# The last tiles of a token pipeline: seven loop passes written out as one order per engine

## The reference, cut to what matters

```python
h = _layernorm(x) * (1 + ca) + sa
x = x + ga * attn(h)            # the token stage
h = _layernorm(x) * (1 + cb) + sb
x = x + gb * experts(h)         # the expert stage
# attn(x):
h = rms_norm(x, ln1_w); xx = shifted(h) - h
r, k, v, g, w = five mixtures of h and xx, each times a matrix
S = dt * S + k * v              # a scan over the tokens, 16 heads of 8 x 8
o = r * (S + u * k * v)         # summed over k
o = groupnorm(o) * gn_w + gn_b
x = x + (o * g) @ Wo
x = x + gelu(rms_norm(x, ln2_w) @ ffn_w1) @ ffn_w2
# experts(x): logits = x @ Wg.T; each token takes its best two of eight experts
```

## Time and the profile before

| | us |
|---|---|
| median of 3 runs | 716.66 (714.81 to 716.93) |
| the profiled execution | 718.54 |
| span of its trace | 716.8 |
| TensorE, VectorE, ScalarE, POOL busy | 618.1, 602.6, 522.4, 536.9 |

### The profile page before, as it was taken

How to read it: one execution, slowest core, us unless ns; L and a number is a source line. 1 busy time by engine, 2 the same in 40 slices (tenths; PEclk the granted TensorE clock), 3 DMA queues, 4 the chain that set the end, 5 groups by cost and what they waited for, 6 DMA issues and landing times. The chain is left out here.

```text
span 716.8 us, 14297 instructions
## 1 busy us (share of the span) xinstructions
PE 618.1 (86%) x3515; PEld 470.7 (66%) x3515; DVE 602.6 (84%) x1384; ACT 522.4 (73%) x1321; POOL 536.9 (75%) x657
## 2 busy tenths in 40 slices
PE   3566789999999989989889777828999999999994
PEld 1433556667777667666667465615888888888883
DVE  6389999999999999997999846566788888888884
ACT  2666578898888957986856576644778878887883
POOL 5457667899999779899969884566588766666666
PEclk9989999999999999999999999957999999999997
DMA  4999888889998897898898799625465444444430
GB/s 109 259 140 133 118 115 134 134 141 157 153 139 155 132 139 121 149 169 148 156 148 151 142 266 290 246 97 152 130 98 86 81 82 81 76 84 80 83 60 1
DMA packets 103300, 95.58 MB, mean 133 GB/s; under 512 B 14523, under 2 KB 82710, under 8 KB 102966
## 3 DMA queue, kind: packets, MB, share of 16 engines
q1 hardware_dynamic: 85846, 79.69, 60.3%
q0 software_dynamic: 16176, 12.75, 9.6%
q10 hardware_dynamic: 1200, 2.23, 0.8%
HBM read 35.47 MB, written 25.61 MB: 85 GB/s over the span
## 5 line engine op out<-in xcount | busy, mean ns | idle before, releaser
L2065 POOL DMA_INDIRECT out<-res,index x91 | 141.4, 1553 | 56.4 <-DVE res L2150 36.5
L843 POOL TENSOR_TENSOR rs_prod<-rT,state_rows 128x512 f32<-128x512 f32 x128 | 139.3, 1097 | 41.0 <-DVE state_rows L1528 39.3
L1281 PEld LDWEIGHTS ps_k<-w,gel 128*128 128x128 f32 x512 | 61.4, 200 | 17.0 <-issue 13.2
L1989 ACT ACTIVATE sig<-ps_a 128x256 f32<-128x256 f32 x91 | 35.1, 385 | 42.8 <-DVE glu L2126 16.9
L1281 PE MATMUL ps_k<-w,gel 128*128 128x128 f32 x512 | 64.1, 286 | 2.4 <-ACT gel L1098 2.4
L1246 PE MATMUL ps_f<-hnT_hi,mix_hi 128*128 128x512 f32 x128 | 55.2, 431 | 8.4 <-DVE hnT_lo L1651 7.6
L2117 DVE SCALAR_TENSOR_TENSOR half<-ps_b,xg,sig 128x256 f32<-128x256 f32 x91 | 43.6, 479 | 21.4 <-ACT sig L1993 18.6
L2110 DVE SCALAR_TENSOR_TENSOR ps_a<-ps_a,xg,sig 128x256 f32<-128x256 f32 x91 | 44.4, 487 | 11.0 <-issue 7.5
L2015 ACT ACTIVATE ps_b<-bias_rows 128x512 f32 x89 | 53.0, 595 | 0.0
L1248 PE MATMUL ps_f<-hnT_hi,mix_lo 128*128 128x512 f32 x128 | 52.2, 408 | 0.0
L1247 PE MATMUL ps_f<-hnT_lo,mix_hi 128*128 128x512 f32 x128 | 52.1, 407 | 0.0
(11 more groups left out here) (357 smaller groups left out, 2000.6 us busy)
## 6 DMA issues: line engine op xcount, KB each, us to landing
v_spread<-vT SPq DMA_DIRECT2D x128, 256.0 KB, 5.3
xg<-sorted_scratch SPq DMA_DIRECT2D x91, 130.0 KB
xin<-in_L_attn_x SPq DMA_DIRECT2D x16, 256.0 KB, 6.3
x<-in_L_attn_x SPq DMA_DIRECT2D x16, 256.0 KB
out<-x SPq DMA_DIRECT2D x16, 256.0 KB
sorted_scratch<-gel SPq DMA_DIRECT2D x4, 910.0 KB, 8.0
tokens_scratch<-h SPq DMA_DIRECT2D x12, 256.0 KB
raw_w<-in_L_ffn_W ACTq DMA_DIRECT2D x2, 1024.0 KB, 9.3
```

The costliest lines, as they stand in the source:

```text
L843: pool.tensor_tensor(rs_prod[:, p, idx % 4], rT[p][:], state[idx][:, p * NT:(p + 1) * NT], ALU.mult).then_inc(s["rs_ready"], 1)
L1281: mm = pe.matmul(ps_k2[:, q * P:(q + 1) * P], gel[c][:, q * P:(q + 1) * P], w2[:, c, :], start=(c == 0), stop=(c == NF - 1))
L2065: pool.indirect_dma_start(out_rows, bass.IndirectOffsetOnAxis(ap=index[k % RESULTS][:, i:i + 1], axis=0), res[k % RESULTS][:, i, :], None, ...
```

## The change

The loop ends after pass 17 (VectorE's after pass 18), and what is left of all tiles is written out in a function `drain()` of each engine, as a list of calls. Pieces of `step` become functions, which loop and list share. Besides the order:

- The feed-forward of tiles 13, 14 and 15 has banks of its own: `h2_bank`, `ffn1_bank` and `ffn2_bank` name them. Before, all but one used `ps_k2` and `ps_m`. The gelus of tiles 13 and 15 go to four tiles in SBUF that are free by then (`gel_late`), the variance of tile 15 to `ps_f[1]`.
- Tiles 14 and 15 reload `x` into the buffers of `vT`, under one semaphore `last_in`.
- The second products of tiles 12 to 14 are issued in two halves, with other work between them.
- The routing of batch 2 is no longer spread over passes: `find_first`, `find_second`, `weigh_shares`, `find_offsets`, `place_rows` are blocks in VectorE's list.
- The second sum of tile 13 (gate and sum with `x`) and the modulation of tile 12 go from POOL to VectorE.
- POOL's listings of batches 0 and 1 stand at other places between its roots; the eight of batch 2 stay last.
- The experts' weights are turned and rounded between the last logits in another order of banks.

The instructions of the passes before are as they were, but for some waits that name one more semaphore.

```diff
-split_banks = ps_f + [key, decay, ps_k2, ps_o]
+split_banks = [ps_f[1], key, decay, ps_k2, ps_o, ps_f[0]]
 SPLIT_BANKS = len(split_banks)
+flat = lambda a: a[:].rearrange("p q d -> p (q d)")
+gel_late = [flat(xin[0]), flat(xin[1]), flat(hn), rT[0][:]]
 w_full = gel + v_spread
...
-MAX_LAG = 9
-ROWS_AT, EXPERTS_AT, SPREAD_AT = TILES + 4, TILES + 3, TILES + 5
-BIAS_ROWS_AT = TILES + 6
-VECTOR_ROWS, VECTOR_GATES = LAST - 2, LAST - 1
+DRAIN = TILES + 2
+assert DRAIN == 18 and LAST == 15 and LISTED == 3
...
-def run_pipeline(step, before):
-    for it in range(TILES + MAX_LAG):
+def run_pipeline(step, before, until=DRAIN):
...
 def h2_bank(t):
-    return key if t == LAST else ps_k2
+    return ps_f[0] if t in (LAST - 2, LAST) else ps_k2
+def ffn1_bank(t, c):
+    late = {LAST - 2: (ps_f[0], key, key, decay), LAST - 1: (ps_k2, key, key, ps_f[1]), LAST: (ps_f[0], ps_f[1], ps_f[1], key)}
+    return late[t][c] if t in late else (ps_k2, ps_m)[c % 2]
+def ffn2_bank(t):
+    return ps_f[0] if t in (LAST - 2, LAST) else ps_k2
+def var_bank(t):
+    return ps_f[1] if t == LAST else ps_k1
+def gel_of(t, c):
+    return gel_late[c] if t in (LAST - 2, LAST) else gel[c][:]
+def x2_of(t):
+    return quarters(vT[t % 2][:]) if t >= LAST - 1 else x2[t % 2]
...
+    def reload(t, p, b):
+        if t < LAST - 1:
+            after(sp, s["xn4_ready"], t - 2)
+            after(sp, s["x2_stored"][p], b - 1, 16, 16)
+        else:
+            after(sp, s["kv_ready"], t, DK, DK)
+            after(sp, s["bonus_ready"], t)
+        sp.dma_start(x2_of(t)[:], x_rows[t]).then_inc(s["last_in"] if t >= LAST - 1 else s["xre_loaded"][p], 16)
+    def renew_late(t, b):
+        after(sp, s["h3_ready"], t - 1)
+        after(sp, s["y_gated"], t - 1)
+        load_late(b + 1)
+    def drain():
+        for idx in range(2, DK):
+            spread_value(idx, LAST, LAST % 2)
+        renew_late(10, 5)
+        store_rows(10, 0)
+        store_sum(11, 1)
+        reload(*at_tile(12))
+        stage_pair(1, 0)
+        stage_pair(1, 1)
+        reload(*at_tile(14))
+        reload(*at_tile(15))
+        stage_batch(1)
+        store_rows(11, 1)
+        store_sum(12, 0)
+        reload(*at_tile(13))
+        renew_late(12, 6)
+        load_last_rows()
+        spread_bias()
+        store_sum(13, 1)
+        load_bias_rows()
+        store_rows(12, 0)
+        store_sum(14, 0)
+        store_rows(13, 1)
+        store_sum(15, 1)
+        store_rows(14, 0)
+        store_rows(15, 1)
...
+    def list_last(first, end):
+        for m in range(first, end):
+            list_pair(LISTED - 1, m)
...
+    def norm_root(t):
+        after(pool, s["ln2_mv"], t)
+        after(pool, s["xn4_ready"], t - 1)
...
+    def drain():
+        scale_rows(*at_tile(10))
+        gate_rows(*at_tile(11))
+        last_products(14, 0)
+        shift_rows(*at_tile(10))
+        first_product(15, 1)
+        list_pair(0, 7)
+        next_products(15, 1)
+        second_root(13)
+        norm_root(11)
+        fifth_product(15, 1)
+        sixth_product(15, 1)
+        last_products(15, 1)
+        number_last()
+        scale_rows(*at_tile(11))
+        shift_rows(*at_tile(11))
+        list_pair(1, 0)
+        gate_rows(*at_tile(12))
+        second_root(14)
+        list_pair(1, 1)
+        second_root(15)
+        norm_root(12)
+        list_pair(1, 2)
+        norm_root(13)
+        list_pair(1, 3)
+        list_pair(1, 4)
+        norm_root(14)
+        norm_root(15)
+        list_pair(1, 5)
+        list_pair(1, 6)
+        list_pair(1, 7)
+        list_last(0, FRONT_EARLY // 2)
...
+    def gelu(t, c):
+        after(act, s["ffn1_ps"][c], t)
+        if t == LAST - 2:
+            act.wait_ge(s["rs_ready"], (LAST - 1) * DK + DK)
+            act.wait_ge(s["hnT_ps"], TILES)
+        if t >= LAST - 1:
+            after(act, s["ffn2_ps"], t - 2)
+        act.activation(gel_of(t, c), ffn1_bank(t, c)[:], ACT.Gelu).then_inc(s["gelu_ready"][c], 1)
+    def keep_second(t):
+        after(act, s["h2T_ps"], t)
+        if t > 0:
+            after(act, s["h2lo_ready"], t - 1)
+            after(act, s["ffn1_ps"][2], t - 1)
+        act.activation(h2T_hi[:], h2_bank(t)[:], ACT.Copy).then_inc(s["h2T_ready"], 1)
+    def drain():
+        keep_second(13)
+        keep_rows(10)
+        gelu(13, 1)
+        gelu(13, 0)
+        keep_logits(10)
+        normalize_second(11, 1)
+        load_experts()
+        gelu(13, 3)
+        gelu(13, 2)
+        head_squares(15)
+        act.preload_act_table_set("natural_log_exp_and_others")
+        head_log(15)
+        head_root(15)
+        second_squares(14)
+        keep_rows(11)
+        second_scale(14)
+        keep_logits(11)
+        keep_second(14)
+        second_squares(15)
+        gelu(14, 1)
+        gelu(14, 0)
+        second_scale(15)
+        gelu(14, 3)
+        gelu(14, 2)
+        keep_second(15)
+        gelu(15, 1)
+        gelu(15, 0)
+        normalize_second(12, 0)
+        gelu(15, 3)
+        gelu(15, 2)
+        exps(2)
+        normalize_second(13, 1)
+        keep_rows(12)
+        keep_totals(2)
+        keep_logits(12)
+        spread_gates()
+        normalize_second(14, 0)
+        keep_rows(13)
+        keep_logits(13)
+        normalize_second(15, 1)
+        keep_rows(14)
+        keep_logits(14)
+        keep_small()
+        round_experts(0, 2)
+        keep_rows(15)
+        round_experts(2, 3)
+        keep_logits(15)
+        round_experts(3, E)
...
+    def ffn2(t, first, end):
+        after(pe, s["gelu_ready"][2], t)
+        after(pe, s["gelu_ready"][3], t)
+        for q in range(first, end):
+            for c in range(NF):
+                mm = pe.matmul(ffn2_bank(t)[:, q * P:(q + 1) * P], gel_of(t, c)[:, q * P:(q + 1) * P], w2[:, c, :],
+                               start=(c == 0), stop=(c == NF - 1))
+        if end == NQ:
+            mm.then_inc(s["ffn2_ps"], 1)
+    def turn_second(t):
+        after(pe, s["h2_ready"], t)
+        turn(h2_bank(t), h2, s["h2T_ps"])
...
+    def drain():
+        pe.wait_ge(s["gelu_ready"][3], 13)
+        pe.wait_ge(s["gelu_ready"][1], 13)
+        turn_rows(10, 0)
+        reduce_even(15, 1)
+        pe.wait_ge(s["silu_set"], TILES)
+        spread_bonus(15)
+        pe.wait_ge(s["expw_ready"], TILES)
+        turn_second(13)
+        ffn2(12, 0, 2)
+        await_second(13)
+        pe.wait_ge(s["kv_ready"], TILES * DK)
+        pe.wait_ge(s["ruk_ready"], TILES)
+        ffn1(13, 1)
+        ffn1(13, 0)
+        score(10)
+        ffn2(12, 2, NQ)
+        pe.wait_ge(s["scan_ready"], TILES * DK)
+        ffn1(13, 3)
+        spread_root(14)
+        reduce_odd(15, 1)
+        after(pe, s["gelu_ready"][1], 13)
+        ffn1(13, 2)
+        join_heads(14)
+        pe.wait_ge(s["bonus_ready"], TILES)
+        variance(15)
+        turn_rows(11, 1)
+        after(pe, s["gelu_ready"][0], 13)
+        ffn2(13, 0, 2)
+        spread_root(15)
+        score(11)
+        ffn2(13, 2, NQ)
+        join_heads(15)
+        after(pe, s["y_ready"], 12)
+        turn_second(14)
+        await_second(14)
+        after(pe, s["gelu_ready"][2], 13)
+        ffn1(14, 1)
+        ffn1(14, 0)
+        ffn1(14, 3)
+        after(pe, s["gelu_ready"][1], 14)
+        ffn1(14, 2)
+        after(pe, s["y_ready"], 13)
+        turn_second(15)
+        after(pe, s["gelu_ready"][0], 14)
+        ffn2(14, 0, 2)
+        await_second(15)
+        after(pe, s["gelu_ready"][3], 14)
+        ffn1(15, 1)
+        ffn1(15, 0)
+        ffn1(15, 3)
+        after(pe, s["gelu_ready"][1], 15)
+        ffn1(15, 2)
+        ffn2(14, 2, NQ)
+        count_classes(2)
+        pe.wait_ge(s["o_ready"], TILES)
+        rank_tokens(2)
+        turn_rows(12, 0)
+        after(pe, s["gelu_ready"][0], 15)
+        ffn2(15, 0, NQ)
+        score(12)
+        add_offsets(2)
+        turn_small()
+        turn_rows(13, 1)
+        turn_experts(0, 2)
+        score(13)
+        turn_experts(2, 5)
+        turn_rows(14, 0)
+        score(14)
+        turn_experts(5, SPLIT_BANKS)
+        turn_rows(15, 1)
+        turn_experts(SPLIT_BANKS, SPLIT_BANKS + 1)
+        score(15)
+        turn_experts(SPLIT_BANKS + 1, E)
+        turn_table()
...
+    def outer_seven(t, p):
+        after(dve, s["v_spread"][3], t, 32, 32)
+        after(dve, s["scan_ready"], t, DK, 6)
+        outer(7, p)
...
+    def find_first(r):
+        dve.wait_ge(s["logits_ready"], (r + 1) * BATCH)
+        dve.wait_ge(s["tag_step"], r * Tagger.STEPS)
+        router.peak(batch_logits(r))
...
+    def drain():
+        middle_scans(15, 1)
+        outer_six(15, 1)
+        scan_six(15, 1)
+        outer_seven(15, 1)
+        rest_second(13)
+        scan_seven(15, 1)
+        better_root(14)
+        add_bonus(15, 1)
+        norm_heads(14)
+        gate_heads(14)
+        sum_heads(15, 1)
+        add_second(12)
+        add_heads(14)
+        better_root(15)
+        norm_heads(15)
+        gate_heads(15)
+        second_stats(12)
```

(38 more changed lines are left out.)

555 lines of the change are left out of this document (305 added, 250 removed).

## The result

The changed kernel took 723.23 us (median of 4 runs, 722.03 to 724.43), where the kernel before took 715.73 beside it (4 runs, 712.87 to 716.93): a ratio of 1.0111, with a 95% interval of 1.0071 to 1.0150. It is slower by some 7.5 us, where a gain was forecast. The profiled execution took 724.43 us, of which 722.7 are the span.

The account below looks back on a forecast made before the run. The drain was taken as bound by waits between engines, with POOL's listing queue ending the token stage. 13.4 less 7.2 gave a gain of 6.2 us: 718.54 - 6.2 + 2.0 = 714.3 profiled, 712.4 median; range 709.3 to 716.8.

Parts of the forecast that it names:

- Second norms: After tile 15's products: norm_root(15) on POOL begins at 449.1 instead of 462.45, 13.4 us earlier.
- Transfers: DMA traffic: same number and size; a late reload(13) covered by VectorE's 1.4 us to spare.
- What is given back: POOL's six listings moved behind norm_root(15): 7.2 us given back; ScalarE's expert rounding hides behind the last eight listings.
- rival (4): Token stage's end: late rounding on ScalarE, not POOL, ends it: 711.8 us; counted within the forecast's 0.66.
- What the schedule leaves out: Drain delays no input explains and low clock stretches: 2.0 us allowed as loss, between none and 7.7.
- The last scans: VectorE's last scan: spread values issued earlier, so it ends near 408.7 instead of 411.88.
- tile 13: TensorE's first product of tile 13 follows the outer products, at 407.7 instead of 413.25.
- Listings: POOL's fourteen listings behind the last root take 18.2 to 19.2 us, 18.7 in the middle.
- The expert stage: Stage behind the barrier: as long as before; a change of its length lay outside the argument.
- Tiles 14 and 15: Feed-forward in the drain: first products at 425.6 and 432.4, distance 6.8 us instead of 15.3, tile 15 11.7 earlier.
- (1): Rival: TensorE's clock falls in the exchange of products and gelus, slower, up to 725.5 us; chance 0.10.
- (2): Rival: norm_root(15) at 455, POOL's fourteen listings behind it eat the gain: 716 us, no change; chance 0.16.

Follow-up runs that it names:

- e5: Changed kernel with a buffer of its own for tile 14's normalized rows, every transfer in its place: 714.97 us, ratio 1.0037 to the kernel before.
- e1: Changed kernel with SyncE's two bias loads issued behind store_rows(13), not ahead of store_rows(12): 724.28 us, ratio 1.0162 to the kernel before.
- e6: Changed kernel without the two bias loads, VectorE writing zeros instead: 717.66 us, ratio 1.0054 to the kernel before.
- e8: Changed kernel with an own buffer for tile 14's rows and listings spread over POOL's waits: 712.75 us, ratio 1.0001 to the kernel before.
- e11: Changed kernel with own buffers for tiles 14 and 15, listings spread, one ScalarE copy fewer for six experts: 711.52 us, ratio 0.9975 to the kernel before.
- e12: Kernel before with only the rounding edit, one ScalarE copy fewer for six experts: 717.03 us, ratio 1.0059 to the unedited kernel before.
- e3: Changed kernel with SyncE issuing reload(13) ahead of store_rows(11): 722.35 us, ratio 1.0120 to the kernel before.
- e4: Changed kernel with store_rows(12) issued by ScalarE on its own DMA queue: 721.52 us, ratio 1.0105 to the kernel before.

## Why the prediction was wrong

**The step that failed** is *Second norms*: "`score(12)` 443.8, `spread_gates` 3.46 on ScalarE until 447.4, then `normalize_second(14)` 1.6: 449.0". I gave `normalize_second(14)` two inputs, a free ScalarE and POOL's root, and left out a third, its buffer, which `store_rows(12)` must have emptied. *Transfers* had "same number and size" and followed SyncE's queue only as far as `reload(13)`, so that the 4 MB of bias loads, which the change puts ahead of that store, appear in no step. Before, the store was issued 22.4 us ahead of its reader (430.86 in that trace, against 453.29). The forecast brought the reader forward to 447.4, and the change put the store back to 442.24, by the place of `normalize_second(12)` in ScalarE's list: 5.2 us apart, in traffic in which the store takes 17.5. The term that it cost is 8.25 us of waiting; e5 takes the wait alone away and gets 7.6 us of the drain back, 5.3 by the ratios; in e1 and e6 it goes with the loads. Whether an earlier `normalize_second(12)` would have been enough, no run tried.

**The second step that failed** is the last sentence of *What is given back*: `round_experts` "hides behind the eight listings". It does not, and this is rival (4), priced at 711.8. POOL's eight listings behind (1, 7) take 10.1 us (e1) to 10.9 (the changed kernel); ScalarE's rounding takes 9.7 us from the landing of (1, 7), and the landing itself 1.6 us behind the last issue in the changed kernel, 2.5 in e5, and 10.7 in e1 beside the bias loads. So ScalarE, not POOL, ends the stage once the store's wait is gone: in e5 by 1.95 us, which is what this term takes there from the gain of 6.2 us, which was POOL's. e5 is at 1.0037, not below 1; the gain came back, as far as it did, only with the listings earlier (e8) and less rounding (e11).

**The third is the base.** The 13.4 us of *Second norms* and the 475.85 to be beaten compare a schedule without delays with a trace that had them. *What the schedule leaves out* counts the late `norm_heads(15)`, the sum that waited "remote" and the low clock in 430 to 432 as risks of the new order, and leaves them in the old one's time. In e12 they are missing: VectorE begins `norm_heads(15)` 0.04 us behind its bank, the sum waits 0.94 us for 2.51, and the clock is 1.00 in 430 to 432. So 4.7 of the 13.4 us (51.8 less 47.1) were delays of the one execution that I read, of which taking the median as 1.9 us lower gave back only a part. Counted from the start of the last scan, the forecast's own end of POOL (469.7, from 407.4) is 62.3 us behind it, 2.5 later than e12's 59.8. So, by an estimate from these two, what POOL could gain was little more than nothing even without the wait for the store: the last scan's 3.2 us less these 2.5. This is one trace against one. That e12's is the more usual of the two, the times suggest: 716.65 us beside a median of 717.03 for e12, where the trace of the rows took 718.54 and the kernel before has medians of 712.65 to 716.66.

**What held.** The last scans, 408.15 + 1.27 = 409.42 for 408.7, and tile 13. Listings: 18.5 us for 18.7. The expert stage took 237.0 us behind the barrier, for 239.2 before; among the other runs it varies from 236.6 to 239.1. *Tiles 14 and 15* was right in kind and too short: tile 14's products came 2.7 us late, with `gelu(13, 3)` 3.23 us behind the issues of `load_experts`, for which I had 1.5; tile 15's came 4.6 late, with VectorE's 3.90 us wait for `reload(13)` ahead of it, where I had found 1.4 to spare. In the changed kernel this is hidden behind the store's wait, as e3 shows. Without the wait it is not: in e5 POOL's last listing ends 65.8 us behind the start of the last scan, 3.5 more than the forecast's 62.3, for the 2.0 us that I had allowed.

**The rivals.** (1) is refuted: the clock was 1.00 in the exchange; the low stretches came behind it, and what ScalarE waited for was a DMA. (2) was nearest: `norm_root(15)` late, with the fourteen listings behind it. Its own rule gives the end well (469.7 plus the 12.6 us by which the root was late is 482.3, for 483.06), but I had put it at "no change", for delays that add up, and had looked for no single one. The case on the slower side was given to the clock alone, and the range of 709.3 to 716.8 ended below the time.

## What to carry to other kernels

When an order is written anew, follow the buffers that come free as well as the inputs: for each instruction moved forward, ask which transfer must have emptied its target, and what that transfer now has ahead of it, on its queue or beside it. Here a store that had been issued 22 us ahead of its reader became the bound when its reader came earlier, its rows came later and a bulk load was issued ahead. When two engines end a stage within 3 us of each other, price both: in e1 POOL was done 10.9 us earlier, and the drain was 0.5 us shorter. And before a gain is read off one trace, see how that execution's time lies among the others: delays that it alone had are no gain of a new order.

## What the runs showed of the hardware

A store of 256 KB landed 17.5 us after its issue behind 4 MB of loads on the same queue, 16.0 in e5, whose transfers have the same places, 14.8 on another queue beside them (e4), and 4.3 and 4.2 without them in flight (e1, e6). The DMA view of e4's stretch from 436 to 470 us has the packets by size:

```profile
DMA packets 5247, 8.06 MB, mean 237 GB/s; under 512 B 409, under 2 KB 4505, under 8 KB 4988
...
q10 hardware_dynamic: 528, 0.26, 2.6%
```

5247 less 4988 are 259 packets of 8 KB or more, which fits 4 MB of bias in 256 pieces of 16 KB; the store, alone on ScalarE's queue (q10: packets, MB, share of the engines), went in pieces of some 500 B. The Trainium skill ("DMA: Bandwidth & Descriptors", section Queues, rings and completion order) says that each of the sixteen engines goes round the queues that it has work for and drains a whole packet, typically some 9 to 17 descriptors, before it switches. If the pieces counted here are such descriptors, which the view does not say, an estimate by that figure gives the store's 33 on an engine two to four turns, and each can stand behind a turn of the loads' 16 KB pieces, so that it would end about when these end, whatever its queue. The two ends, 457.8 and 437.49 + 19.9 = 457.4, agree with that. It is argued from the counts and not shown: no run changed the size of the pieces.

In e6 one of POOL's listings lasted 4.44 us, from 466.82 to 471.26, across VectorE's second zero write (466.41 to 469.88), while two others under the first (462.14 to 465.61) kept their 0.96. One case does not settle whether the write held it.
